# Layer 4's first two layer norms done batch by batch inside layer 3's closing part, and a projection matrix multiplied into the up matrix

## The reference, cut to what matters

```python
# layer 3: the end of its mixer (rms_norm divides each row by its root mean square), y = what its scan left
y = y @ Wproj.T
x = x + y + jnp.square(jax.nn.relu(rms_norm(y) @ Wfc.T)) @ Wcp.T + experts     # experts: two per token
# layer 4: a norm, and inside the feed-forward part a second one on the first one's output
xn  = (x - mean(x)) / jnp.sqrt(var(x) + 1e-05)
xln = (xn - mean(xn)) / jnp.sqrt(var(xn) + 1e-05) * ln1_w + ln1_b
att_out = jax.nn.sigmoid(xln @ Wr) * (xln @ Wv) @ Wo
rwkv_state = xln @ Ws
h = third_norm(xn + att_out)
```

## Time and profile before

| | us |
|---|---|
| three runs | 2260.11, 2262.36, 2264.63; median 2262.36 |
| span of the profiled execution | 2259.2 |
| PE busy | 1884.8 (83%) |
| DVE busy | 1639.0 (73%) |
| ACT busy | 1200.9 (53%) |
| POOL busy | 594.0 (26%) |
| mean granted TensorE clock | 0.901 |

### The profile page before, as it was taken

The page is one execution under the profiler, slowest core; times in us unless marked ns, Lnnn a source line. Parts: engine busy times, 40 slices in busy tenths (PEclk is TensorE's granted clock), DMA queues, the critical chain, the costliest instruction groups (busy, mean ns, idle before and its releaser), DMA issues. The chain is left out here.

```text
span 2259.2 us, 45441 instructions
## 1 busy us (share of the span) xinstructions
PE 1884.8 (83%) x17701; PEld 999.6 (44%) x17701; DVE 1639.0 (73%) x2739; ACT 1200.9 (53%) x2431; POOL 594.0 (26%) x675
## 2 busy tenths in 40 slices
PE   2878887866647999999979799999789979887987
PEld 1222221443311335953333277767464434555755
DVE  5999999675779997579863855545766768876366
ACT  2999999332333885258755255546422420221475
POOL 1112110011675542125434623330224000000160
PEclk7899899987676999999988899999779989998986
DMA  8423420100461433734221112221002342430310
GB/s 278 85 57 82 86 59 1 75 18 6 111 208 31 119 58 94 211 61 70 36 31 48 54 60 66 71 65 45 11 30 68 93 124 88 137 92 13 117 52 33
DMA packets 156414, 172.01 MB, mean 76 GB/s; under 512 B 55308, under 2 KB 124886, under 8 KB 156194
## 3 DMA queue, kind: packets, MB, share of 16 engines
q1 hardware_dynamic: 142616, 144.18, 23.4%
q0 software_dynamic: 13584, 24.92, 4.5%
HBM read 95.73 MB, written 77.28 MB: 77 GB/s over the span
## 5 line engine op out<-in xcount | busy, mean ns | idle before, releaser
L443 ACT ACTIVATE a_E<-a_scores,a_nmax 128x512 f32<-128x512 f32 x512 | 343.7, 829 | 13.8 <-DVE a_nmax L376 12.6
L1022 ACT ACTIVATE a_E<-a_scores 128x512 f32<-128x512 f32 x512 | 273.6, 600 | 96.3 <-PE a_scores L1057 91.3
L376 DVE TENSOR_REDUCE a_nmax<-a_scores 128x2 f32<-128x1024 f32 x256 | 303.6, 1219 | 20.4 <-PE a_scores L458 15.7
L926 DVE TENSOR_REDUCE a_nmax<-a_first 128x2 f32<-128x1024 f32 x256 | 295.7, 1219 | 14.4 <-PE a_first L1047 13.3
L458 PE MATMUL a_scores<-a_Vh,a_Kh 48*128 48x512 bf16 x512 | 107.1, 416 | 97.9 <-ACT a_E L443 73.7
L1047 PE MATMUL a_first<-a_Kh,a_Qh 48*128 48x512 bf16 x512 | 147.5, 415 | 38.0 <-PEq L51 21.2
L471 PE MATMUL a_turn<-a_E,a_QS 128*32 128x256 f32 x2048 | 173.0, 414 | 2.2 <-DVE a_QS L386 1.8
L443 ACT ACTIVATION_READ_ACCUMULATOR a_E<-a_scores,a_nmax 128x1 f32 x512 | 173.8, 349 | 0.0
L1057 PE MATMUL a_scores<-a_Qh,a_Kh 51*128 51x512 bf16 x512 | 161.0, 395 | 5.0 <-PEq L51 1.9
L1079 PE MATMUL a_out<-a_E,a_V 128*32 128x256 f32 x2048 | 162.1, 397 | 0.0
L458 PEld LDWEIGHTS a_scores<-a_Vh,a_Kh 48*128 48x128 bf16 x512 | 24.9, 94 | 218.1 <-ACT a_E L443 178.3
(11 more groups left out here) (581 smaller groups left out, 4402.4 us busy)
## 6 DMA issues: line engine op xcount, KB each, us to landing
f_up<-in_L_up SPq DMA_DIRECT2D x32, 256.0 KB, 3.3
a_Kh<-a_rows_k SPq DMA_DIRECT2D x16, 384.0 KB, 6.0
a_Vh<-a_rows_v SPq DMA_DIRECT2D x16, 384.0 KB, 9.5
a_Qh<-a_rows_q SPq DMA_DIRECT2D x32, 192.0 KB, 5.0
a_Kh<-a_rows_k SPq DMA_DIRECT2D x32, 192.0 KB, 5.3
slots<-empty SPq DMA_DIRECT2D x8, 645.0 KB, 6.4
f_xe<-slots SPq DMA_DIRECT2D x40, 129.0 KB
outs<-zeros SPq DMA_DIRECT2D x8, 512.0 KB, 5.8
```

Source lines behind the costliest of these rows:

```text
L376: v.tensor_reduce(nmax[:, rd % 2, r1, :, q], bank(b, u)[:], AX.X, ALU.max, negate=True).then_inc(S["max_ready"], 1)
L443: m = a.activation(E[:, u % NE, x], bank(b, u)[:, x], ACT.Exp, bias=nmax[:, rd % 2, r1, x, q:q + 1], accum_out=Z[:, rd % 2, r1, x, q:q + 1])
L926: v.tensor_reduce(out, slot_bank(n)[:], AX.X, ALU.max, negate=True).then_inc(S["slot_read"], 1)
L1022: a.activation(E[:, u % NE, x], ps_s[n % 3][:], ACT.Exp, scale=SCALE).then_inc(S["exp_ready"], 1)
```

## The change

`finish2` takes over the norms "3" and "3a". The projection matrix is turned (`WpT`) and multiplied into the up matrix once, at the start (`Wup`), and the up products read the scan's output `yT` directly; `ps_p` and `ypT` go. Per batch DVE takes the statistics as before and then the two variances (`statistics`), ACT one square root for both (`root`), DVE the reciprocal and the second norm's rows (`norm`, into `rows2`), POOL the first norm's rows (into `g.XN`); for the last batch DVE does three tiles of these and POOL one. PE turns both, one after the other, in one PSUM buffer (`turn_rows2`, `turn_xn`, `ps_t`), and ACT moves them out (`take_rows2`, `take_xn`). `combine` now comes before `add_mlp`. In `ffn3` both norms go, and SP's `load_weights` moves to the start of the mixing block. A table load for the square root stands at the start of `finish2`, one for the sigmoid at the start of the mixing block. The transposed second norm's output, `HT`, becomes a tensor that lives from layer 3 on and is used again later for `MS`; storage of layer 3 is given back earlier for it.

```diff
-        ypT = k.sb("a2_ypT", [C, 2, T])
+        WpT, Wup = k.sb("a2_WpT", [C, C]), k.sb("a2_Wup", [C, NF * 128])
...
+        lvar, lstd, lroot = (k.sb(f"a2_l{n}", [128, NB, 2, R]) for n in ("var", "std", "root"))
+        rows2 = k.sb("a2_rows2", [128, 2, R, C])
...
-        ps_p = k.ps("a2_ps_p", [128, T])
...
+        ps_t = k.ps("a2_ps_t", [128, R, 128])
...
+        def normalise(eng, out, kind, b, r):
+            n, s = divmod(b * R + r, 2)
+            return eng.tensor_scalar(out, g.X[:, b, r], g.stats[:, n, s, 1:2], lroot[:, b, kind, r:r + 1],
+                                     ALU.subtract, ALU.mult)
...
-                    if b:
-                        pe.wait_ge(S["p_read"], b)
-                    pe.matmul(ps_p[:], Wp[:], yT[:, b], start=True, stop=True).then_inc(S["p_done"], 1)
...
                 def up_products(b):
-                    pe.wait_ge(S["p_read"], b + 1)
                     for f in range(NF):
                         i = b * NF + f
                         if i >= 3:
                             pe.wait_ge(S["f_read"], i - 2)
-                        pe.matmul(ps_f[i % 3][:], Wfc[:, f * 128:(f + 1) * 128], ypT[:, b % 2], start=True, stop=True
+                        pe.matmul(ps_f[i % 3][:], Wup[:, f * 128:(f + 1) * 128], yT[:, b], start=True, stop=True
...
+                def turn_rows2(b):
+                    pe.wait_ge(S["rows2_ready"], b + 1)
+                    if b:
+                        pe.wait_ge(S["xt_read"], b)
+                    for r in range(R):
+                        m = pe.transpose(ps_t[:, r], rows2[:, b % 2, r], g.ident[:])
+                    m.then_inc(S["ht_turned"], 1)
+
+                def turn_xn(b):
+                    pe.wait_ge(S["xn_ready"], b + 1)
+                    if b == NB - 1:
+                        pe.wait_ge(S["xn_last"], 1)
+                    pe.wait_ge(S["ht_read"], b + 1)
+                    for r in range(R):
+                        m = pe.transpose(ps_t[:, r], g.XN[:, b, r], g.ident[:])
+                    m.then_inc(S["xt_turned"], 1)
...
                 pe.wait_ge(weights_loaded, 3 * 16)
+                pe.transpose(ps_m[0][:, 0:C], Wp[:], g.ident[:]).then_inc(S["wp_turned"], 1)
                 project(0)
+                pe.wait_ge(S["wp_read"], 1)
+                pe.matmul(ps_m[1][:], WpT[:], Wfc[:], start=True, stop=True).then_inc(S["up_made"], 1)
+                project(1)
+                pe.wait_ge(S["up_ready"], 1)
                 for b in range(NB):
-                    if b + 1 < NB:
+                    if 0 < b < NB - 1:
                         project(b + 1)
                     up_products(b)
+                    if b >= 3:
+                        turn_xn(b - 3)
                     if b:
                         down_products(b - 1)
+                    if b >= 2:
+                        turn_rows2(b - 2)
+                turn_xn(NB - 3)
                 down_products(NB - 1)
+                for b in (NB - 2, NB - 1):
+                    turn_rows2(b)
+                    turn_xn(b)
...
+                def root(b):
+                    a.wait_ge(S["var_ready"], b + 1)
+                    a.activation(lstd[:, b], lvar[:, b], ACT.Sqrt).then_inc(S["std_ready"], 1)
+
+                def take_rows2(b):
+                    a.wait_ge(S["ht_turned"], b + 1)
+                    a.activation(g.HT[:, b], ps_t[:].rearrange("c r p -> c (r p)"), ACT.Identity, scale=ln_cols[:, 0:1],
+                                 bias=ln_cols[:, 1:2]).then_inc(S["ht_read"], 1)
+
+                def take_xn(b):
+                    a.wait_ge(S["xt_turned"], b + 1)
+                    a.activation(g.XT[:, b].rearrange("c (p r) -> c p r", r=R), ps_t[:].rearrange("c r p -> c p r"),
+                                 ACT.Identity).then_inc(S["xt_read"], 1)
...
                 def taken(b):
-                    a.wait_ge(S["p_done"], b + 1)
-                    if b >= 2:
-                        a.wait_ge(S["f_done"], b * NF - NF)
-                    a.copy(ypT[:, b % 2], ps_p[:]).then_inc(S["p_read"], 1)
                     a.wait_ge(S["y_done"], b + 1)
...
+                a.activation(g.unit_root[:], g.ident[:, 0:1], ACT.Sqrt)
+                a.wait_ge(S["up_made"], 1)
+                a.copy(Wup[:], ps_m[1][:]).then_inc(S["up_ready"], 1)
                 taken(0)
                 for b in range(NB):
                     if b + 1 < NB:
                         taken(b + 1)
+                    if b >= 3:
+                        take_rows2(b - 3)
                     for f in range(NF):
                         i = b * NF + f
+                        if f == NF - 1 and b >= 2:
+                            root(b - 2)
                         a.wait_ge(S["f_done"], i + 1)
                         if f == 0 and b >= 2:
                             a.wait_ge(S["m_done"], b - 1)
                         a.activation(hr[:, b % 2, f], ps_f[i % 3][:], ACT.Relu).then_inc(S["f_read"], 1)
                         a.drain()
                         a.activation(hr[:, b % 2, f], hr[:, b % 2, f], ACT.Square).then_inc(S["h_ready"], 1)
-                a.activation(g.unit_root[:], g.ident[:, 0:1], ACT.Sqrt)
+                    if b >= 3:
+                        take_xn(b - 3)
+                root(NB - 2)
+                take_rows2(NB - 3)
+                take_xn(NB - 3)
+                take_rows2(NB - 2)
+                take_xn(NB - 2)
+                root(NB - 1)
+                take_rows2(NB - 1)
+                take_xn(NB - 1)
...
+            @block.gpsimd
+            def _(pool):
+                for b in range(NB):
+                    pool.wait_ge(S["root_ready"], b + 1)
+                    for r in range(R - 1 if b == NB - 1 else 0, R):
+                        m = normalise(pool, g.XN[:, b, r], 0, b, r)
+                    m.then_inc(S["xn_ready"], 1)
...
+
+                def statistics(b):
                     pair_statistics(v, g, g.X, b)
+                    v.drain()
+                    var = g.stats[:, b * R // 2:(b + 1) * R // 2, :, 2:3].rearrange("p n s o -> p (n s o)")
+                    v.tensor_scalar(lvar[:, b, 0], var, 1.0 / C, EPS, ALU.mult, ALU.add)
+                    v.tensor_scalar(lvar[:, b, 1], var, (1.0 + EPS) / C, EPS * EPS, ALU.mult, ALU.add
+                                    ).then_inc(S["var_ready"], 1)
+
+                def norm(b):
+                    v.wait_ge(S["std_ready"], b + 1)
+                    v.reciprocal(lroot[:, b], lstd[:, b]).then_inc(S["root_ready"], 1)
+                    v.drain()
+                    if b >= 2:
+                        v.wait_ge(S["ht_turned"], b - 1)
+                    for r in range(R):
+                        m = normalise(v, rows2[:, b % 2, r], 1, b, r)
+                    m.then_inc(S["rows2_ready"], 1)
+                    if b == NB - 1:
+                        for r in range(R - 1):
+                            m = normalise(v, g.XN[:, b, r], 0, b, r)
+                        m.then_inc(S["xn_last"], 1)
...
+                v.wait_ge(S["wp_turned"], 1)
+                v.tensor_copy(WpT[:], ps_m[0][:, 0:C]).then_inc(S["wp_read"], 1)
                 add_y(0)
                 for b in range(NB):
                     if b + 1 < NB:
                         add_y(b + 1)
+                    v.drain()
+                    combine(b)
+                    if b:
+                        norm(b - 1)
                     add_mlp(b)
-                    combine(b)
+                    statistics(b)
+                norm(NB - 1)
...
-        HT = k.sb("f3_HT", [C, NB, T])
+        HT = g.HT
...
-            layer_norm(nc, g, "3", g.X, g.XN, g.XT, ahead=load_weights, again=True)
-            g.recycle_sems()
-            layer_norm(nc, g, "3a", g.XN, rows, HT, scale=ln_cols[:, 0:1], bias=ln_cols[:, 1:2], by_row=True)
...
             with nc.Block(no_gpsimd_drain=True) as block:
+                @block.sync
+                def _(sp):
+                    load_weights(sp)
+
                 @block.tensor
...
                 @block.scalar
                 def _(a):
+                    a.activation(g.unit_root[:], g.ident[:, 0:1], ACT.Sigmoid)
                     for b in range(NB):
...
-        MS, OT = k.sb("a3_MS", [C, NB, T]), k.sb("a3_OT", [C, NB, T])
+        MS, OT = g.HT, k.sb("a3_OT", [C, NB, T])
...
             if s == "ln2":
                 until_l2.close()
+                g.HT = g.sb("HT", [C, NB, T])
```

More of the change, by code:

```diff
@@ L2492, in finish2 @@
         Wp, Wfc, Wcp = weights
-        ypT = k.sb("a2_ypT", [C, 2, T])
+        WpT, Wup = k.sb("a2_WpT", [C, C]), k.sb("a2_Wup", [C, NF * 128])
         sq = k.sb("a2_sq", [128, 2, R, C])
         ms, inv = k.sb("a2_ms", [128, 2, R]), k.sb("a2_inv", [128, 2, R])
+        lvar, lstd, lroot = (k.sb(f"a2_l{n}", [128, NB, 2, R]) for n in ("var", "std", "root"))
+        rows2 = k.sb("a2_rows2", [128, 2, R, C])
         hr = k.sb("a2_hr", [128, 2, NF, T])
```

(21 more changed lines are left out.)

## The result

The changed kernel took 2245.27 us (median of eight runs, 2238.71 to 2252.91), the kernel before 2260.79 in the same set (eight runs, 2256.35 to 2281.32). The ratio is 0.993 with a 95% interval of 0.991 to 0.995: faster by 0.5 to 0.9%. Forecast were 2249.5, 0.57% less. The direction came true. The forecast's ratio lies inside the interval, so whole times do not tell the larger gain from the forecast one. The profiled execution has a span of 2243.8 and a time of 2245.6.

What follows compares the result with a forecast made beforehand. TensorE was taken to bound the rounds, followed by 25.2 us of serial norms. Start, rounds, tail, border and load put the mixing at 1607.7, 12.9 us earlier: span 2246.3, plus 3.2 gives 2249.5 us (-0.57%), range 2245.0 to 2254.5.

Steps and rivals of the forecast that it cites:

- S to first up product: From PE's first instruction of the closing part: turn, projections and merged up matrix at half clock, 4.5 us.
- first up product to E: The rounds of the closing part, full ones 8.99 us and PE's, through down product 6: 63.7 us.
- E to last eviction's end: The tail after down product 6: PE's wait, down product 7, last statistics, roots, turns and evictions, 17.4 us.
- load: Mixing weights at the border, 320 KB from issue to landing: 2.6 us, upper end 5.0.
- the tail's clock: Down product 7, after about 3 us of PE idle time, runs partly at half clock: 1.5 us more.
- rival (a): PE keeps full clock in the tail, 1.5 less for down product 7, 0.9 in turns: 2247.1 us; chance 0.2.
- the middle 0.55: Price of one group of four PE turns in a round, taken between bounds 0.45 and 0.66 us.
- The frame: Whole time: profiled span forecast 2246.3 us, plus 3.2 for the median above the span, gives 2249.5.
- (b): A round becomes VectorE's (+2.5 us) or the mixing load lands late (+2.4), both 2254.4 us; chance 0.22 together.
- (c): VectorE and GpSimd block each other when normalising, 3.3 us longer a round: 2268 us, slower; chance 0.04.
- (d): Moved work saves little: down product 7's wait spreads to every round, five lose 2.9 each, 2264.0 us; chance 0.04.
- The price of the order: Tail: PE turns batch 5's first norm before down product 7 and so waits; 2.9 us lost to the order.

Runs made afterwards that it cites:

- e0: The changed kernel run once more, nothing altered: 2252.85 us; first up product to end of last eviction 78.67 us against 78.55.
- e1: Changed kernel with the mixing weights loaded earlier, in the closing part: last eviction to mixing's first product 1.24 us against 5.44.
- e4: Changed kernel with SyncE waiting for the mixing weights before issuing the seven loads behind them: 4.17 us from issue to PE's start.
- e6: Changed kernel with GpSimd's share of the first norm done by VectorE: first up product to last eviction's end 84.19 us against 78.55.
- e3: Changed kernel with VectorE's combine of batch 7 ahead of batch 6's statistics: down product 7 took 4.70 us against 3.74.
- e10: Unread PE turns filling tail gaps, added to changed kernel with early load, down product 7 and last root moved ahead, another PSUM buffer: ratio 0.992 to kernel before.
- e2: Changed kernel with down product 7 issued ahead of batch 5's first-norm turn: first up product to last eviction's end 78.61 us against 78.55.
- e8: e2 with batch 7's root ahead of the eviction of batch 6's first norm: first up product to last eviction's end 77.34 us.

## Why the prediction came out as it did

The sum, term by term (predicted, then the changed kernel):

| term | predicted | measured |
|---|---|---|
| S to first up product | 4.5 | 4.44 |
| first up product to E (end of down product 6: 1581.56 + 3.57) | 63.7 | 62.73 |
| E to last eviction's end | 17.4 | 15.82 |
| border | 1.46 | 1.19 |
| load | 2.6 | 4.25 |

**The mechanism was right in the rounds and at the border.** 25 us of serial norms vanished under rounds that stayed PE's; the rounds pay nothing, a tail and a bare load stay. VectorE fitted with 0.86 to spare (0.7 forecast), and the wait ahead of down product 7 is 2.73 (3 forecast).

**The step that failed is the tail's clock**: "At the start of this part 4.14 us of idle was followed by 3 us at half clock; I expect much the same here, so +1.5". Down product 7 took 3.74 at clock 1.00, so this term was 0, and E to the end of down product 7 took 7.71 (1592.84 less E), not 9.3. That is one half of rival (a), to which I gave 0.2. Its other half, 0.9 less for turns, did not come: two groups took 0.60 and 0.63, but the last two 1.01 and 1.09, and from down product 7 to the last eviction it was 8.11 where the sum had 8.1. So the whole error of the tail, 1.6, is this one term. The analogy took one gap for another: after 2.73 (again in e0, e1 and e4) the clock stood, after 3.76 (e6) and 5.26 (e3) it had fallen. But the length of the last gap is not all that counts. The last two groups fell to 0.50 behind gaps of 2.23 and 0.96, with little other work before them, and with those gaps filled the clock stayed at 1.00 (e10). In e6, with a wait one microsecond longer, the term was 2.3, more than I gave it.

**Mis-sized terms.** A group of four turns is 0.44, the lower bound that I had worked out, not the middle 0.55: ten groups, 1.1 us, which is the rounds' 1.0. The load is 4.25, not 2.6: I priced bytes moved, but PE waits for the signal, and e4 shows 1 us from the issue to the first data and 1.7 us between the last data and the start; the upper end that I kept, 5.0, was nearer. The Trainium skill, "DMA: Bandwidth & Descriptors", section "Anatomy of one DMA — SWDGE (gpsimd) path", gives a fixed cost of about 2 us beside the bytes, most of it behind the last byte, for transfers that GpSimd issues. That is the shape that e4 shows for one that SyncE issues; by the page's fit 328 thousand bytes would take 2.75 us, an estimate, where the runs took 3.78 to 4.41. The errors of the table cancel in part: -1.0 in the rounds, -1.6 in the tail, -0.3 at the border and +1.65 for the load give a start of the mixing 1.2 earlier than the sum had it.

**The frame.** I added 3.2 us, the median of the runs less one profiled span. Of the same execution time and span differ by 1.8 (2245.6 and 2243.8; 1.7 to 2.9 in the eight runs): the other 1.4 were a difference between executions, not an offset. Of the 4.2 us between forecast and median, the sum explains 1.2 and this 1.4. Of the remaining 1.6, 0.2 lie ahead of S, 0.3 between the profiled execution and the median, and 1.1 behind M, where the changed kernel's execution took 637.4 and that of the kernel before 638.6. "All that follows shifts along" holds only to within what executions differ.

**The rivals.** (b) didn't come as a whole: no round became VectorE's, but its late load came by 1.65 of the 2.4. (c), mutual exclusion of VectorE and GpSimd, is refuted: 1.11 beside GpSimd, 1.12 without it (e6). The Trainium skill, "SBUF — State Buffer", section "Who interferes with whom", allows such an exclusion for tensor_scalar; it did not occur here. (d) is refuted: PE's round is 8.78 without idle time.

**The price of the order.** The prediction said that 2.9 us were lost to it. 1.5 of these were the half clock that did not come; the other 1.4 are VectorE's wait for down product 7, 1.36 in the row of 1593.05. e2 shows that removing this wait alone gives nothing, and e8 that 1.2 to 1.3 are to be had once the root behind GpSimd's rows is moved as well.

## What to carry to other kernels

When serial work is moved under a loop, look at what it had been hiding: here a load issued 24 us ahead became a bare 4 us at the border, and issuing it earlier gave back more (4.2) than any other edit. Price a load on the path from issue to the waiter's start, not by bytes over bandwidth. In an in-order tail one wait hides the next: after an order is mended, look for the instruction that is queued behind the following one (e2, then e8). Measure edits of a few microseconds between landmarks of the trace, and check first that the landmarks repeat.
